# A graph network on one core: rows of y scattered behind later gathers, and the hub's scores turned through two PSUM banks

## The chip, the cores and the metric

The kernel runs on one core of a Trainium2 chip. The time is the device time of one launch in microseconds, from the first to the last instruction with what lies around it. The kernel before has a median of 2826.6 us in three runs (2820.92 to 2831.66). One execution was taken by the hardware profiler; all rows below are from it, in microseconds from the start of its span.

## What is computed

The graph has 8192 nodes with 128 features and a 0/1 adjacency matrix of 8192 x 8192 with ones on its diagonal. Its first nodes have many neighbours and its last ones a few.

```python
def reference(x, adj, W0, b0, a_s, a_r, W1, b1):
    # layer 0: attention over the neighbours
    h = maximum(layernorm(x), 0)
    H = h @ W0.T + b0
    s, r = H @ a_s, H @ a_r
    e = leaky_relu(adj * s + adj * r.T, 0.2)
    x = x + softmax(where(adj > 0, e, -9e15), axis=1) @ H
    # layer 1: sum over the neighbours, then the largest over the neighbours
    h = maximum(layernorm(x), 0) @ W1
    p = maximum(adj @ h + b1, 0)
    return x + max_over_neighbours(p, adj)
```

Below, y is `layernorm(x)` of layer 1 after its maximum, times W1: one row of y per node.

## The kernel before

The 8192 rows are 64 tiles of 128. Tile 0, the hub, is dense and has its own path; the other 63 are sparse. **Layer 0** reads the adjacency matrix tile by tile in the order STREAM, packs each row's bits on TensorE (`pack`), and VectorE takes the numbers of the neighbours out of them (`extract`). Rows are then sorted by their number of neighbours in four groups (`rank_group` on POOL, behind VectorE's ranks), so that tile q of the ranked order needs A_SLOTS[q] gathers: each gather (L589) is one indirect DMA of 128 rows of `h_table` into a slot of the ring of 64 slots.

All engines run the same list of steps, n = 0 to 76, and meet by semaphores. STEP[q] says at which step ranked tile q is scored. In step n ScalarE normalizes the tiles of step n - 2 (`tile_normalize`), copies their transposes (`tile_copies`, L790), writes their rows of y (`tile_rows`, L803), then makes the raw scores of this step's tiles (`raw_scores`, L747). VectorE finishes scores (L1314, which gathers four tiles later wait for), and TensorE sums the slots one step later (`sum_slots`, L976).

POOL's order is written out: for q = 0 to 62 the gathers of tile q, and behind them the scatters (L602) of the tiles m with BEHIND[m] = q. Before the tiles 0, 16, 27 and 47 it ranks a group (L575). A scatter of tile m waits for the row of y of step STEP[m] + 2; a gather of tile q waits for the scores of tile q - 4 and for free slots. POOL works in order, so what stands behind a waiting scatter waits with it.

The hub's scores are made by VectorE in steps 64 to 67 and become exponents on ScalarE. In the steps 68 to 71 they are turned and multiplied in 16 chunks of 4 blocks, four chunks a step. For chunk c TensorE transposes four blocks into PSUM (`dense_transpose`, L1016), ScalarE copies them to SBUF (`dense_keep`, L817) and TensorE multiplies them with 512 rows of `h_table` (`dense_sum`, L1023), which SP loads (L437) into one of two buffers once the sum two chunks before is done. The order on TensorE is transposes of c, then sum of c - 1. Step 72 closes the hub (`dense_close`, L1370 on) and gives its row of y.

**Layer 1** then splits y in three bf16 parts (`split_y`, L1392 on), multiplies the packed words of tiles 1 to 27 and the hub on TensorE (L1093), while POOL gathers y for the rest (L624); at last POOL gathers the results (L661) and VectorE takes the largest (L1330).

Of the kernel before, what the change touches and what calls it, by code (L numbers as in the profile page):

```python
# [7 lines left out]
ALU, ACT, AX = mybir.AluOpType, mybir.ActivationFunctionType, mybir.AxisListType  # L8

P = 128  # L10
# [6 lines left out]
BANK = 512  # L17
VSCALE = 4096.0
BATCH = 4
BATCHES = T // BATCH  # L20
# [69 lines left out]
def gathered_by(slots):  # L90
# [21 lines left out]
STEP = [18, 19, 20, 20, 21, 22, 22, 23, 24, 24, 25, 25, 26, 26, 27, 27, 34, 38, 40, 41, 42, 43, 44, 45, 46, 46,  # L112
    47, 53, 54, 55, 55, 56, 57, 57, 58, 58, 59, 60, 60, 61, 61, 62, 62, 63, 63, 64, 64, 65, 66, 67, 68, 68,
    69, 69, 70, 70, 71, 71, 72, 72, 73, 73, 74]
BEHIND = [5, 6, 8, 8, 9, 11, 11, 12, 14, 14, 16, 16, 17, 17, 17, 17, 20, 21, 23, 24, 25, 26, 27, 27, 30, 30, 31,
    32, 33, 35, 35, 36, 38, 38, 40, 40, 41, 44, 44, 47, 47, 47, 47, 49, 49, 51, 51, 52, 53, 54, 56, 56, 58,
    58, 61, 61, 62, 62, 62, 62, 62, 62, 62]
HUB_SCORES, HUB_SUMS, HUB_NORM = T, T + 4, T + 8
LAST = max(STEP[-1] + 2, HUB_NORM + 1)
AT_STEP = {n: [q for q in range(NR) if STEP[q] == n] for n in range(-3, LAST + 1)}  # L120
SCATTER_BEHIND = {n: [q for q in range(NR) if BEHIND[q] == n] for n in range(NR)}

# [39 lines left out]
def build(nc, x, adj, W0, b0, a_s, a_r, W1, b1, out):  # L162
    ctx = ExitStack()
    with ctx:
        def sb(name, shape, dt=F32):
            return ctx.enter_context(nc.sbuf_tensor(name, shape, dt))

        def ps(name, shape, dt=F32):
            return ctx.enter_context(nc.psum_tensor(name, shape, dt))

        def sem(name):
            return ctx.enter_context(nc.semaphore(name))
# [13 lines left out]
        a_buf = sb("a_buf", [P, 2, N])  # L186
# [47 lines left out]
        ident = sb("ident", [P, P])  # L234
# [31 lines left out]
        hn = [sb(f"hn{i}", [P, BATCH, D]) for i in range(2)]  # L266
        hT = [sb(f"hT{i}", [P, BATCH, P]) for i in range(2)]
# [51 lines left out]
        psV = [ps(f"psV{i}", [P, WORDS]) for i in range(2)]  # L319
        psF = ps("psF", [P, BANK])  # L320
        psW = psF[:].bitcast(BF16)
        psT = ps("psT", [P, BATCH, P])
        psH = [ps(f"psH{i}", [P, BANK]) for i in range(2)]
        psA = [psV[i][:, 0:BANK] for i in range(2)]

        s_xin, s_w, s_b1, s_c0, s_c1, s_c2, s_const, s_waug, s_waug_sb, s_held, s_constants = (
# [29 lines left out]
        s_hin, s_htr, s_hwt, s_hmm, s_hst = (  # L356
            [sem(f"{n}{l}") for l in range(3)] for n in ("s_hin", "s_htr", "s_hwt", "s_hmm", "s_hst"))
# [323 lines left out]
        def _(act):  # L681
# [131 lines left out]
            def dense_keep(l, t, c):  # L813
                act.wait_ge(s_htr[l], t * BATCHES + (c + 1))
                if c >= 2:
                    act.wait_ge(s_hmm[l], t * BATCHES + (c - 1))
                act.activation([hn[1], hT[1]][c % 2][:].rearrange("p u n -> p (u n)"), psF[:], ACT.Copy).then_inc(  # L817
                    s_hwt[l], 1)

            def dense_norm(l, t):  # L820
# [13 lines left out]
            for n in range(LAST + 1):  # L834
# [33 lines left out]
                if HUB_SUMS <= n < HUB_NORM:  # L868
                    for c in range(4 * (n - HUB_SUMS), 4 * (n - HUB_SUMS) + 4):
                        dense_keep(0, 0, c)  # L870
# [23 lines left out]
            with act.If(general(act) > 0):  # L894
                with act.Fori(0, T) as t:
                    dense_exponents(1, t)
                    for c in range(BATCHES):
                        dense_keep(1, t, c)
                    dense_norm(1, t)
                with act.Fori(0, T) as t:  # L900
                    for c in range(BATCHES):
                        dense_keep(2, t, c)

        @block.tensor
        def _(pe):
# [101 lines left out]
            def dense_transpose(l, t, c):  # L1007
                if l == 2:
                    pe.wait_ge(s_hin[2], (t + 1) * 16)
                else:  # L1010
                    pe.wait_ge(s_hexp[l], t * PLANES + (c // 2 + 1))
                if c >= 1:
                    pe.wait_ge(s_hwt[l], t * BATCHES + c)
                for j in range(BATCH):
                    at = (c * BATCH + j) * P
                    last = pe.transpose(psF[:, j * P:(j + 1) * P], a_buf[:, 0, at:at + P], ident[:])  # L1016
                last.then_inc(s_htr[l], 1)

            def dense_sum(l, t, c):
# [15 lines left out]
            for n in range(LAST + 1):  # L1035
# [26 lines left out]
                if HUB_SUMS <= n < HUB_NORM:  # L1062
                    if n == HUB_SUMS:
                        pe.wait_ge(s_wt, DENSE)
                        pe.wait_ge(s_onehot, 4)
                    for c in range(4 * (n - HUB_SUMS), 4 * (n - HUB_SUMS) + 4):
                        dense_transpose(0, 0, c)
                        if c > 0:
                            dense_sum(0, 0, c - 1)
# [13 lines left out]
            for c in range(DENSE_BATCHES):  # L1083
                if c >= 2:
                    pe.wait_ge(s_relu, c - 1)
                for i, b in enumerate(BLOCK_ORDER):
# [3 lines left out]
                    for k in range(PLANES):  # L1090
                        at = (b * PLANES + k) * D
                        for part in range(3):
                            last = pe.matmul(psA[c % 2], y_part[part][:, at:at + D],  # L1093
                                             bit_rows[(c * BLOCKS + i) % 3][:, k, :],
                                             start=(i == 0 and k == 0 and part == 0),
                                             stop=(i == BLOCKS - 1 and k == PLANES - 1 and part == 2))
# [7 lines left out]
            with pe.If(general(pe) > 0):  # L1104
                with pe.Fori(0, T) as t:
                    for c in range(BATCHES):
                        dense_transpose(1, t, c)
                        if c > 0:
                            dense_sum(1, t, c - 1)
                    dense_sum(1, t, BATCHES - 1)  # L1110
                    dense_norm(1, t)
                with pe.Fori(0, T) as t:
                    for c in range(BATCHES):
                        dense_transpose(2, t, c)
                        if c > 0:
                            dense_sum(2, t, c - 1)
                    dense_sum(2, t, BATCHES - 1)
# [497 lines left out]
```

## Time and profile before

| | us |
|---|---|
| median of 3 runs | 2826.6 |
| lowest, highest | 2820.92, 2831.66 |
| the profiled execution | 2835.18 |
| its span | 2826.0 |
| mean granted TensorE clock | 0.669 |

A row of the order of time gives start, duration, engine, line, operation, output and input, the number of instructions merged in it, and in brackets how long the engine stood idle before it and what released it. "issue" means that nothing was waited for that the profile shows; "remote" that the releaser isn't known. The ends of matmuls are modelled.

### The profile page before, as it was taken

How to read it: one execution, taken by the hardware profiler on the slowest of the kernel's cores; microseconds unless marked ns; L12 is line 12 of the kernel's file. 1: busy time of each engine (PE TensorE's matmuls, PEld its weight loads, DVE VectorE, ACT ScalarE, POOL GpSimd, SP SyncE). 2: the span in 40 equal slices, each digit the busy share in tenths (PEclk: the TensorE clock that was granted, in tenths of full speed). 3: DMA queues.
4: the chain of work that ended last, by engine and by line, in shares of the span. 5: the costliest groups of instructions: out<-in, count | busy, mean ns of one | idle time of the engine just before them, and what ended most of it. 6: DMA issues, size and time to landing. Idle time of an engine off the chain costs nothing.

```text
span 2826.0 us, 19035 instructions
## 1 busy us (share of the span) xinstructions
PE 968.4 (34%) x4534; PEld 535.7 (19%) x4534; DVE 1438.5 (51%) x3301; ACT 456.3 (16%) x1519; POOL 1562.0 (55%) x1616
## 2 busy tenths in 40 slices
PE   3664156525245536423539996600000000000000
PEld 1431133213122213323514432300000000000000
DVE  6888677855334525443265543547656345222222
ACT  1631145302123214433410000000000000000000
POOL 0102755444664645576363564677766755677776
PEclk8987577767677768666759997855555555555555
DMA  9999668788567879632441221152232111222121
GB/s 351 410 381 375 189 239 291 283 224 321 194 241 244 297 261 387 212 79 70 120 97 40 75 61 48 51 132 59 67 56 43 52 42 40 48 57 54 49 47 41
DMA packets 155983, 447.42 MB, mean 158 GB/s; under 512 B 34557, under 2 KB 81459, under 8 KB 122970
## 3 DMA queue, kind: packets, MB, share of 16 engines
q1 hardware_dynamic: 80506, 311.94, 29.2%
q0 software_dynamic: 53184, 114.44, 16.9%
q10 hardware_dynamic: 22176, 19.77, 2.3%
q8 instruction: 38, 0.62, 0.1%
q14 instruction: 79, 0.65, 0.1%
HBM read 408.06 MB, written 37.95 MB: 158 GB/s over the span
## 4 chain that ended last, share of the span: by engine, by line
another core or an unknown queue 20%; POOL 18%; PE 16%; issue 15%; DVE 11%; DMA 6%; DVEq 6%; ACT 4%; SPq 2%; ACTq 1%; POOLq 0%
POOL ring L661 16%; PE psV L1093 9%; DMA a_buf<-in_adj 5%; PE psV L920 3%; DVE squares L1330 2%; SPq L390 2%; ACT ring L764 2%; POOL out L667 1%; PE psH L976 1%; DVE a_buf L1495 1%; DVEq L1499 1%; DVE words L1221 1%; DVE words L1212 1%; DVEq L1215 1%
## 5 line engine op out<-in xcount | busy, mean ns | idle before, releaser
L589 POOL DMA_INDIRECT ring<-h_table,srec x518 | 506.5, 978 | 304.0 <-issue 170.3
L661 POOL DMA_INDIRECT ring<-p_table,srec x545 | 529.8, 972 | 200.3 <-issue 166.9
L920 PE MATMUL psV<-a_buf,bit_ident 128*128 128x512 bf16 x1024 | 318.4, 476 | 245.7 <-DMA a_buf<-in_adj 173.8
L1330 DVE TENSOR_REDUCE squares<-ring 128x128 f32<-128x640 f32 (+15 forms) x99 | 178.0, 1798 | 333.4 <-DMA ring<-p_table,srec 301.9
L976 PE MATMUL psH<-ring,ident 128*128 128x128 f32 x1036 | 159.3, 316 | 205.9 <-remote 93.2
L624 POOL DMA_INDIRECT ring<-y_table,srec x198 | 191.8, 969 | 62.4 <-issue 61.8
L1093 PE MATMUL psV<-rec_all,a_buf 128*128 128x512 bf16 x888 | 202.0, 385 | 26.0 <-issue 25.9
L1103 PE MATMUL psH<-ones_row,flag_col 128*1 128x1 f32 x2 | 0.2, 163 | 589.7 <-DVEq L1556 589.7
L920 PEld LDWEIGHTS psV<-a_buf,bit_ident 128*128 128x128 bf16 x1024 | 115.5, 115 | 432.3 <-issue 296.0
L976 PEld LDWEIGHTS psH<-ring,ident 128*128 128x128 f32 x1036 | 149.6, 228 | 220.2 <-issue 205.9
L1314 DVE SCALAR_TENSOR_TENSOR e_sc<-e_sc 128x6 f32<-128x6 f32 (+19 forms) x63 | 10.7, 170 | 259.1 <-ACT e_sc L748 245.0
L764 ACT ACTIVATE ring<-ring,prob 128x128 f32<-128x128 f32 x433 | 131.9, 389 | 5.4 <-issue 3.9
L1458 DVE TENSOR_SCALAR rec_all<-a_buf 128x512 uint16<-128x512 uint16 x296 | 67.6, 301 | 122.7 <-remote 73.9
L1093 PE MATMUL psV<-wbuf,a_buf 128*128 128x512 bf16 x456 | 113.6, 399 | 47.5 <-issue 25.9
L575 POOL DMA_INDIRECT records<-rec_all,rank x63 | 61.4, 974 | 98.6 <-DVEq L1302 80.6
L1212 DVE MAX8 words<-psV 128x8 f32<-128x1024 f32 x63 | 77.7, 1233 | 71.9 <-remote 49.4
L1093 PEld LDWEIGHTS psV<-rec_all,a_buf 128*128 128x128 bf16 x888 | 87.6, 99 | 136.8 <-issue 36.1
L1103 PEld LDWEIGHTS psH<-ones_row,flag_col 128*1 128x1 f32 x2 | 0.1, 80 | 590.0 <-issue 590.0
L661 POOL DMA_INDIRECT ring<-p_table,w_aug x93 | 87.8, 944 | 36.0 <-issue 28.0
L631 POOL DMA_INDIRECT p_table<-rec_all,srec x36 | 35.8, 994 | 123.3 <-DVEq L1447 117.7
L564 POOL DMA_DIRECT2D h_table<-stage x16 | 12.3, 766 | 160.6 <-ACT rs_col L713 160.6
L602 POOL DMA_INDIRECT y_table<-rec_all,srec x36 | 36.0, 1001 | 116.9 <-ACT rec_all L803 110.8
(228 smaller groups left out, 2055.5 us busy)
## 6 DMA issues: line engine op xcount, KB each, us to landing
a_buf<-in_adj SPq DMA_DIRECT2D x256, 1024.0 KB
ring<-p_table,srec POOLq DMA_INDIRECT x545
ring<-h_table,srec POOLq DMA_INDIRECT x518
trec<-records ACTq DMA_DIRECT2D x63, 128.5 KB
packed<-wbuf ACTq DMA_DIRECT2D x28, 256.0 KB
a_buf<-packed SPq DMA_DIRECT2D x7, 1024.0 KB
h_table<-stage POOLq DMA_DIRECT2D x16, 258.0 KB, 7.6
a_buf<-r_row SPq DMA_DIRECT2D x1, 4096.0 KB
```

Of the source, the lines that this page charges most:

```text
L390: sp.dma_start(a_buf[:, n % 2, cols], adj[STREAM[n] * P:(STREAM[n] + 1) * P, cols]).then_inc(s_a[n % 2], 16)
L575: pool.indirect_dma_start(records[g], bass.IndirectOffsetOnAxis(rank[:, g, i:i + 1], 0), rec[g][:, i, :], None).then_inc(s_rec, 16)
L589: pool.indirect_dma_start(ring[:, A_AT[q] + j, :], None, h_table, bass.IndirectOffsetOnAxis(srec_u[g][:, i, LIST + j:LIST + j + 1], 0)).th ...
L624: pool.indirect_dma_start(ring[:, Y_AT[m] + j, 0:D], None, y_table, bass.IndirectOffsetOnAxis(srec_u[g][:, i, LIST + j:LIST + j + 1], 0)). ...
L661: pool.indirect_dma_start(ring[:, C_AT[n] + j, 0:D], None, p_table, bass.IndirectOffsetOnAxis(slot, 0)).then_inc(s_rows[n % BUFS], 16)
L764: act.activation(row, row, ACT.Copy, scale=prob[q % 2][:, j:j + 1])
L920: last = pe.matmul(psV[n % 2][:, h * BANK:(h + 1) * BANK].rearrange("p (g n) -> p g n", n=P), bit_ident[:, k, :], rows[:, :, k, :], start= ...
L976: pe.matmul(psH[q % 2][:, 0:D], ident[:], ring[:, A_AT[q] + j, 0:D], start=(j == 0), stop=False)
L1093: last = pe.matmul(psA[c % 2], y_part[part][:, at:at + D], bit_rows[(c * BLOCKS + i) % 3][:, k, :], start=(i == 0 and k == 0 and part == 0 ...
L1212: dve.max(words[:, 0:8], src)
L1330: dve.tensor_reduce(to, ring[:, at:at + n, 0:D].rearrange("p s d -> p d s"), AX.X, op)
L1458: last = dve.tensor_scalar(bit_rows[n % 3][:, k, :].bitcast(U16).rearrange("p (u n) -> p u n", n=P), words_in[c % 2][:, :, b * P:(b + 1) * ...
```

## The change

The list BEHIND is changed for 18 tiles: the scatters of the tiles 7 to 9, 31 to 38 and 49 to 55 stand behind the gathers of later tiles, by 2 to 49 gathers. Tiles 8 and 9 go past the second ranking to behind tile 16, tiles 37 and 38 past the fourth ranking to behind tile 47.

In the hub's chunks the transposes of even chunks go to the bank psF as before and those of odd chunks to the first bank of psV[1]. The transposes of chunk c wait for the copy of chunk c - 2 instead of that of chunk c - 1.

```diff
-BEHIND = [5, 6, 8, 8, 9, 11, 11, 12, 14, 14, 16, 16, 17, 17, 17, 17, 20, 21, 23, 24, 25, 26, 27, 27, 30, 30, 31,
-    32, 33, 35, 35, 36, 38, 38, 40, 40, 41, 44, 44, 47, 47, 47, 47, 49, 49, 51, 51, 52, 53, 54, 56, 56, 58,
-    58, 61, 61, 62, 62, 62, 62, 62, 62, 62]
+BEHIND = [5, 6, 8, 8, 9, 11, 11, 13, 16, 16, 16, 16, 17, 17, 17, 17, 20, 21, 23, 24, 25, 26, 27, 27, 30, 30, 31,
+    32, 33, 35, 35, 37, 39, 39, 41, 41, 44, 47, 47, 47, 47, 47, 47, 49, 49, 51, 51, 52, 53, 56, 58, 58, 61,
+    61, 62, 62, 62, 62, 62, 62, 62, 62, 62]
...
+        psX = [psF, psV[1]]
...
-                act.activation([hn[1], hT[1]][c % 2][:].rearrange("p u n -> p (u n)"), psF[:], ACT.Copy).then_inc(
+                act.activation([hn[1], hT[1]][c % 2][:].rearrange("p u n -> p (u n)"), psX[c % 2][:, 0:BANK], ACT.Copy).then_inc(
...
-                if c >= 1:
-                    pe.wait_ge(s_hwt[l], t * BATCHES + c)
+                if c >= 2:
+                    pe.wait_ge(s_hwt[l], t * BATCHES + c - 1)
                 for j in range(BATCH):
                     at = (c * BATCH + j) * P
-                    last = pe.transpose(psF[:, j * P:(j + 1) * P], a_buf[:, 0, at:at + P], ident[:])
+                    last = pe.transpose(psX[c % 2][:, j * P:(j + 1) * P], a_buf[:, 0, at:at + P], ident[:])
```

## Rows read from the trace of the kernel before

**Rows 1.** The page: busy time of each engine, and the chain that ended last.
```profile
PE 968.4 (34%) x4534; PEld 535.7 (19%) x4534; DVE 1438.5 (51%) x3301; ACT 456.3 (16%) x1519; POOL 1562.0 (55%) x1616
...
another core or an unknown queue 20%; POOL 18%; PE 16%; issue 15%; DVE 11%; DMA 6%; DVEq 6%; ACT 4%; SPq 2%; ACTq 1%; POOLq 0%
```
**Rows 2.** Table of stretches: us, busy per engine, TensorE clock, DMA share, GB/s.
```profile
1448.00:1855.00 407.00, 313.08 (x1372) 136.59 (x1370) 190.09 (x601) 8.58 (x14) 221.24 (x228) 0.86 0.23 62
1855.00:2826.00 971.00, 0.19 (x2) 0.11 (x2) 407.92 (x508) 0.00 (x0) 676.78 (x695) 0.50 0.23 54
```
**Rows 3.** POOL in order of time, 1317 to 1390 us.
```profile
1317.43 0.94 POOL L589 DMA_INDIRECT ring<-h_table,srec  x1 [0.30 <-issue]
1332.43 0.98 POOL L602 DMA_INDIRECT y_table<-rec_all,srec  x1 [14.06 <-ACT rec_all L803]
...
1342.48 0.94 POOL L589 DMA_INDIRECT ring<-h_table,srec  x1 [0.30 <-issue]
...
1380.89 0.94 POOL L589 DMA_INDIRECT ring<-h_table,srec  x1 [0.30 <-issue]
```
**Rows 4.** ScalarE in order of time, the hub's copies, 1321 to 1384 us.
```profile
1321.34 0.60 ACT L817 ACTIVATE hn<-psF 128x512 f32<-128x512 f32 x1 [12.99 <-remote]
...
1334.99 0.57 ACT L817 ACTIVATE hn<-psF 128x512 f32<-128x512 f32 x1
1336.69 0.60 ACT L817 ACTIVATE hT<-psF 128x512 f32<-128x512 f32 x1 [1.13 <-PE psF L1016]
...
1345.23 0.60 ACT L817 ACTIVATE hT<-psF 128x512 f32<-128x512 f32 x1 [4.40 <-remote]
...
1383.02 0.60 ACT L817 ACTIVATE hT<-psF 128x512 f32<-128x512 f32 x1 [5.76 <-remote]
```
**Rows 5.** Waits of 1302:1430 (us, times, longest); then L790: what ended ScalarE's idleness.
```profile
ACT hT L817 <- remote: 15.3, 3, 5.8
...
  remote: 143.4, 15
```
**Rows 6.** TensorE and SP in order of time, 1307 to 1325 us.
```profile
1307.51 1.91 PE L1023 MATMUL psV<-stage,hn 128*128 128x128 f32 x8
1309.21 1.06 PE L1016 MATMUL psF<-ident,a_buf 128*128 128x128 f32 x4
...
1321.28 0.91 SPq L437 DMA_DIRECT2D stage<-h_table  x2
...
1324.24 2.04 PE L1023 MATMUL psV<-stage,hn 128*128 128x128 f32 x8 [1.07 <-DMA stage<-h_table]
```
**Rows 7.** POOL: two scatters and two rankings in time, then waits of 1110:1192 and 1302:1392.
```profile
480.06 0.98 POOL L602 DMA_INDIRECT y_table<-results,srec  x1 [3.98 <-ACT results L803]
499.25 0.97 POOL L602 DMA_INDIRECT y_table<-results,srec  x1 [6.95 <-ACT results L803]
518.12 0.98 POOL L575 DMA_INDIRECT records<-rec_all,rank  x1 [12.80 <-DVEq L1302]
...
1195.99 0.99 POOL L575 DMA_INDIRECT records<-rec_all,rank  x1 [2.65 <-DVEq L1302]
...
POOL y_table L602 <- ACT rec_all L803: 22.5, 5, 8.8
...
POOL y_table L602 <- ACT rec_all L803: 36.6, 4, 14.1
```
**Rows 8.** ScalarE and VectorE in order of time: scores of later tiles.
```profile
1246.10 0.32 ACT L747 ACTIVATE e_sc<-ring,srec 128x14 f32<-128x14 f32 x1 [14.10 <-DMA ring<-h_table,srec]
...
1264.32 0.17 DVE L1314 SCALAR_TENSOR_TENSOR e_sc<-e_sc 128x9 f32<-128x9 f32 x1 [2.45 <-issue]
...
1333.29 0.17 DVE L1314 SCALAR_TENSOR_TENSOR e_sc<-e_sc 128x6 f32<-128x6 f32 x1 [24.34 <-ACT e_sc L748]
```
**Rows 9.** VectorE and TensorE in order of time, from the hub's close to layer 1.
```profile
1394.54 0.16 DVE L1370 TENSOR_REDUCE hub_inv<-hub_l 128x1 f32<-128x8 f32 x1
...
1447.89 2.72 PE L1093 MATMUL psV<-wbuf,a_buf 128*128 128x512 bf16 x6 [20.97 <-DVE wbuf L1458]
```

## The prediction

> **What bounds the kernel now.** I read the page first, then the table of stretches, then the order of time engine by engine. The page says that no engine is full: POOL is busy for 55% of the span, VectorE for 51%, TensorE for 34% [rows 1]. The chain of the page splits in the same way, with a fifth of it put down to nothing that the profile can name [rows 1]. So the change has to be judged where it works, and the rest of the kernel counts only as something that is shifted. The table of stretches shows this: from 1855 us to the end only POOL and VectorE work, POOL for 677 of 971 us, and TensorE's long stage lies between 1448 and 1855 us [rows 2]. Neither holds an edited instruction. They begin when layer 0 is done, so what the change is worth is what it does to the end of layer 0, the hub's close and the first product of layer 1.
>
> That start is set by the hub. Its close on VectorE begins at 1394.54; behind it come the hub's row of y, the loads of y and twelve splits on VectorE before the first unpacking, and TensorE starts at 1447.89 [rows 9]. Ahead of 1394.54 stand the steps 68 to 71, each with four chunks of the hub's scores. Once in each of them ScalarE's copy waits for something that the profile can't name: 12.99 us in step 68, and 15.3 us in three waits in the steps 69 to 71 [rows 4, 5]. I read these waits beside POOL's order. The last gather of a run ends at 1318.37 (1317.43 + 0.94), 1343.42 and 1381.83 [rows 3], and the copies start at 1321.34, 1345.23 and 1383.02 [rows 4], 2.97, 1.81 and 1.19 us later. Step 70 looks alike. Layer 0 as a whole has 15 more such waits at L790, 143.4 us of ScalarE [rows 5]. TensorE's own records of the work waited for are much earlier: the third group of transposes is drawn at 1309.21 with 1.06 us, the copy that waits for it starts at 1321.34, and SP's loads, of which one waits for the sum drawn at 1307.51, leave at 1321.28 [rows 4, 6]. Two engines agree on the late time, so the late time is the real one. The Trainium skill (Perfetto Trace Analysis, the per-instruction lifecycle of the Tensor Engine) says that the end drawn for TensorE is an estimate; by that reading the trace agrees, the lag here being 11 us.
>
> **The change part by part.**
> *The hub's banks.* No operation is added or removed: 64 transposes and 16 copies stay. Before, a group of transposes waits for the copy of the group ahead, and the copy then waits for the transposes: the copy at 1334.99 takes 0.57, and the next one starts at 1336.69 [rows 4]. With two banks the transposes of an odd chunk are done ahead, and the second copy can follow at once: 1336.69 - 1335.56 = 1.1 us per step at most, for the pair that isn't held. But the sum of a chunk still waits for its rows: the load that leaves at 1321.28 lets the sum start at 1324.24 [rows 6], two chunks behind. And the last copy of steps 68 to 71 is held by the unnamed wait in any case. From below zero I exclude: psV[1] is free from step 64 on, as TensorE waits for the last turned words. Bounds 0 and 4 x 1.1 = 4.4 us of gain; I take 1, because three of four steps end in the unnamed wait, and in step 71 I expect part of it to be free.
>
> *The rows of y.* 18 scatters move behind 2 to 49 later gathers. On POOL that takes away 11 waits: 3.98 and 6.95 us in the first group, five with 22.5 us in the third, four with 36.6 us in the fourth, 70.0 us in all [rows 3, 7]. Each scatter is still 0.98 us and each gather 0.94, with 0.30 between them, near 1.3 and 1.25 us [rows 3], so POOL's work is the same. Where do the 70 us go?
> In the first group the wait is followed by one for VectorE's ranks, 12.80 us before the first record of the second group [rows 7]: the gain ends there, 0. In the third group there is the same wait, 2.65 us [rows 7]; ranks come from step 62, and step 62 isn't reached sooner by gathers that already run two steps ahead of the scores. I take 0 with bounds of -3 and +3, the wait that can be used up.
> Scatters 37 and 38 move past the fourth group's ranks to behind gather 47, where four others stand already. That puts 2 x 1.3 = 2.6 us ahead of gather 48. Rows are waited for here: ScalarE stood 14.10 us before tile 47's, and VectorE 2.45 us before the score of tile 48, with only hub scores behind it [rows 8]. This cost is on the path: +2.6.
> In the fourth group a gather still waits for the score of the tile four before it. So POOL doesn't run away: without the scatter of tile 49 it goes on to gather 55 (4 gathers, 5.0 us) and then stands before gather 56 until the score of tile 52, made at 1333.29, 0.9 us behind the scatter's start at 1332.43 [rows 3, 8]. If TensorE's completion comes only behind the run of gathers, then that run now ends 5.0 us later in step 68: +5.0. In step 69 the run is four gathers, a scatter and four gathers as before (11.3 us) but starts behind the score: with the drain and POOL's own start I take +1.5. In step 70 it is three gathers, two scatters, three gathers, 10.1 instead of 11.35 us, and starts later by the same: +0.3. In step 71 it is five gathers and two scatters, 8.9 instead of 12.6 us: -3.7 + 1.5 = -2.2.
> Sum: 2.6 + 5.0 + 1.5 + 0.3 - 2.2 = +7.2, less 1 for the banks: +6.2 us. The profiled execution has a span of 2826.0 us and took 2835.2 us, 0.3% above the median of 2826.6 us; a shift of 6 us carries over whole, so 2826.6 + 6 = about 2832 us.
>
> A rule speaks against the reading on which this rests. The Trainium skill (SBUF — State Buffer, "Who interferes with whom") says that a DMA written by POOL is held only by VectorE's shared port and that a DMA never contends with another engine. By it TensorE's late completions have nothing to do with the runs, and a longer run costs nothing, which is the second rival. The rows above don't agree with it, as far as a coincidence of three times can tell.
>
> **The rivals.**
> *The waits turn into time.* The 36.6 us that POOL loses in the fourth group are real idle time of the engine that otherwise holds TensorE. If gathers done early leave TensorE alone when the hub's chunks come, each of the four steps loses part of its unnamed wait, 12.99 us and 15.3 us in three [rows 4, 5]. Two thirds of step 68's and half of the others would be 8.7 + 7.6 = 16 us: 2826.6 - 16 = 2811. For it: those waits are large. Against it: the score of the tile four back keeps POOL's work inside the same steps.
> *Nothing is coupled.* The unnamed waits have another origin and stay; POOL's waits were free. Then only the banks act, 3 us of the 4.4, and scatters 37 and 38 hide: 2824. Against it: the runs' ends and the waits' ends lie together too often. For it: nothing that I know of makes TensorE wait for POOL's DMAs.
> *Slower.* The hold isn't given back. Where a run grows, TensorE's sums that begin in it wait for its end: tile 13's gathers (5, 6.25 us) before scatter 7, tile 37's (5, 6.25 us) before scatter 31, tile 55's (5.0 us) before scatter 49, and 2.6 us for scatters 37 and 38: 20 us, 2847. It decides from the point where later runs, though shorter, end no sooner, because their start hangs on the score, which itself comes behind the hold.
> *The change doesn't do what it says.* VectorE and ScalarE keep TensorE from using the second bank and the scatters wait where the gathers did: 2827.
>
> **How the numbers follow.** Coupled, with the hold given back in part (2832): 0.50. Nothing coupled (2824): 0.20. Waits turn into time (2811): 0.14. Slower (2847): 0.12. No effect (2827): 0.04. The median's own spread is 2820.9 to 2831.7. For 8 in 10 the range has to reach over the centre of the fast rival and most of the slow one: 2811 to 2846. About 0.5% (14 us) is what a measurement of this kernel can tell from no change. Faster by more than that: over half of the fast rival, 0.09. Slower: three quarters of the slow one and the tail of the forecast, 0.12. Between them 0.79.
>
> **What would show it.** The run behind gather 54 goes on with gather 55, and the copy of step 68 that stood at 1321.34 comes 5 to 8 us later, again behind the last gather. POOL's waits ahead of L602 in the fourth group shrink below 15 us and stand ahead of L589 instead, with the scores as releaser. VectorE's hub close moves from 1394.54 to about 1401, TensorE's first product from 1447.89 to about 1454. In the first pair of a step's hub copies the second follows the first within 0.1 us, where it took 1.1 us. It would be wrong if those copies come in the middle of a run of gathers, if the third group's ranks move by more than 3 us, or if anything behind 1455 us changes its length.

## The result and the profile after

The changed kernel has a median of 2835.55 us in 20 runs (2820.82 to 2842.82), the kernel before 2827.38 us in 20 runs. The ratio is 1.0023 with a 95% interval of 1.0013 to 1.0033: 6.5 us slower, between 3.7 and 9.3 (the two medians lie 8.2 us apart). The forecast was +6.2 us, about 2832 us. The profiled execution took 2841.26 us, its span is 2833.2 us, against 2835.18 and 2826.0 us before. Line numbers of the changed kernel are higher by 1.

The page of the changed kernel, busy times and the chain that ended last, as [rows 1]:

```profile
PE 973.4 (34%) x4534; PEld 537.1 (19%) x4534; DVE 1438.1 (51%) x3301; ACT 457.0 (16%) x1519; POOL 1566.3 (55%) x1616
...
issue 20%; POOL 19%; PE 17%; another core or an unknown queue 12%; DVE 11%; DMA 6%; DVEq 5%; ACT 5%; SPq 4%; ACTq 1%; POOLq 0%
```

The busy times are within 5 us of those of before, with the same counts of instructions: nothing was added. The unnamed share of the chain fell from 20% to 12%, and that of "issue" rose from 15% to 20%. Then the two last stretches, as [rows 2] (the second is longer by the longer span):

```profile
1448.00:1855.00 407.00, 310.84 (x1372) 136.21 (x1372) 190.55 (x603) 8.67 (x14) 225.25 (x232) 0.86 0.24 62
1855.00:2833.00 978.00, 0.19 (x2) 0.11 (x2) 407.80 (x508) 0.00 (x0) 675.82 (x692) 0.50 0.23 54
```

POOL in order of time where its list was changed most, as [rows 3]:

```profile
1330.19 0.95 POOL L590 DMA_INDIRECT ring<-h_table,srec  x1 [0.30 <-issue]
1344.69 0.95 POOL L590 DMA_INDIRECT ring<-h_table,srec  x1 [13.55 <-DVEq L1318]
...
1348.44 0.95 POOL L590 DMA_INDIRECT ring<-h_table,srec  x1 [0.30 <-issue]
...
1361.73 0.95 POOL L590 DMA_INDIRECT ring<-h_table,srec  x1 [6.02 <-DVEq L1318]
...
1377.35 0.95 POOL L590 DMA_INDIRECT ring<-h_table,srec  x1 [5.80 <-DVEq L1318]
```

The run goes on to gather 55 and ends at 1331.14; then POOL stands before gather 56 until the score of tile 52. The later runs too begin behind a score. Of the 36.6 us that POOL waited ahead of L602 between 1302 and 1392 [rows 7] nothing is left ahead of its scatters there; it waits 31.1 us ahead of gathers instead, each time for a score. ScalarE's copies beside them, as [rows 4] and [rows 5]:

```profile
1313.66 0.58 ACT L818 ACTIVATE hn<-psF 128x512 f32<-128x512 f32 x1
1314.13 0.59 ACT L818 ACTIVATE hT<-psV 128x512 f32<-128x512 f32 x1
1334.70 0.60 ACT L818 ACTIVATE hn<-psF 128x512 f32<-128x512 f32 x1 [19.98 <-remote]
1335.20 0.59 ACT L818 ACTIVATE hT<-psV 128x512 f32<-128x512 f32 x1
...
1345.20 0.58 ACT L818 ACTIVATE hn<-psF 128x512 f32<-128x512 f32 x1
...
1350.35 0.60 ACT L818 ACTIVATE hT<-psV 128x512 f32<-128x512 f32 x1 [2.29 <-remote]
...
1357.70 0.45 ACT L791 ACTIVATE hT<-psT 128x128 f32<-128x128 f32 x2 [3.47 <-remote]
...
1368.84 0.60 ACT L818 ACTIVATE hT<-psV 128x512 f32<-128x512 f32 x1 [4.08 <-remote]
...
1381.64 0.60 ACT L818 ACTIVATE hT<-psV 128x512 f32<-128x512 f32 x1 [1.25 <-PE psV L1017]
```

In step 68 the unnamed wait grew from 12.99 to 19.98 us and again ends behind the run, by 3.56 us. In the steps 69 to 71 the hub's share of it shrank: 15.3 us in three waits became 2.29 + 4.08. Another 3.47 us stand now ahead of the copies for the rows of y (L791), where this stretch had none before; they end 2.0 us behind the run whose last gather ends at 1355.71. So part of the wait only changed its place. The odd copies follow the even ones by 0.5 us, start to start. VectorE's hub close and TensorE's first product, as [rows 9], moved by 0.4 and 0.3 us only, where 6 to 7 us had been forecast for both:

```profile
1394.94 0.16 DVE L1371 TENSOR_REDUCE hub_inv<-hub_l 128x1 f32<-128x8 f32 x1
...
1448.19 6.64 PE L1094 MATMUL psV<-wbuf,a_buf 128*128 128x512 bf16 x24 [21.10 <-DVE wbuf L1459]
```

So in this pair of executions 6.8 of the 7.2 us between the spans lie behind the close: 2826.0 - 1394.54 = 1431.5 us before, 2833.2 - 1394.94 = 1438.3 after. The hub's steps began 7.75 us later (1313.66 against 1305.91) and were 7.35 us shorter together. One execution of each can't say whether that is the change; the runs below say how much this stretch varies.

### The profile page after: what moved, and what is told of

The parts are those of the page before. It is cut to its first block, busy times and chain, and to the rows that moved or that the text cites. A ratio compares the mean times of both kernels' runs of the same rounds, so it can differ in the third digit from the quotient of the medians.

```text
span 2833.2 us, 19034 instructions
## 1 busy us (share of the span) xinstructions
PE 973.4 (34%) x4534; PEld 537.1 (19%) x4534; DVE 1438.1 (51%) x3301; ACT 457.0 (16%) x1519; POOL 1566.3 (55%) x1616
## 4 chain that ended last, share of the span: by engine, by line
issue 20%; POOL 19%; PE 17%; another core or an unknown queue 12%; DVE 11%; DMA 6%; DVEq 5%; ACT 5%; SPq 4%; ACTq 1%; POOLq 0%
POOL ring L662 15%; PE psV L1094 10%; DMA a_buf<-in_adj 4%; PE psV L921 2%; DVE squares L1331 2%; SPq L391 2%; PE psH L977 2%; POOL out L668 1%; ACT ring L765 1%; SPq L404 1%; DVE a_buf L1496 1%; DVEq L1500 1%; DVE a_buf L1486 1%; POOL records L576 1%
## 5 line engine op out<-in xcount | busy, mean ns | idle before, releaser
L921 PE MATMUL psV<-a_buf,bit_ident 128*128 128x512 bf16 x1024 | 326.6, 485 | 236.3 <-DMA a_buf<-in_adj 145.9
L1213 DVE MAX8 words<-psV 128x8 f32<-128x1024 f32 x63 | 77.7, 1233 | 60.0 <-remote 49.3
L668 POOL DMA_INDIRECT out<-results,srec x63 | 64.1, 1018 | 52.1 <-DVEq L1532 33.8
```

The costliest lines, as they stand in the source:

```text
L668: pool.indirect_dma_start(out, bass.IndirectOffsetOnAxis(srec_u[g][:, i, ROW:ROW + 1], 0), results[:, n % RESULTS, :], None).then_inc(s_re ...
L921: last = pe.matmul(psV[n % 2][:, h * BANK:(h + 1) * BANK].rearrange("p (g n) -> p g n", n=P), bit_ident[:, k, :], rows[:, :, k, :], start= ...
L1213: dve.max(words[:, 0:8], src)
```

## The experiments

The experiments were run in four groups on three chips, and these are of two kinds: on two of them the kernel before takes 2485 us, on the third 2853 us; on that of the first pair it took 2827 us. Each ratio is against the kernel before, run on the same chip at the same time. The lists BEHIND are given by the tiles whose scatters are at their new place.

**The banks alone (e1), the list alone (e2), the tiles 7 to 9 alone (e3), 49 to 55 alone (e4).**

```diff
# e1: psX as in the change, BEHIND as before
# e2: BEHIND as in the change, psF alone as before
# e3: only these of BEHIND
-..., 12, 14, 14, ...   (tiles 7, 8, 9)
+..., 13, 16, 16, ...
# e4: only these of BEHIND
-..., 54, 56, 56, 58, 58, 61, 61, ...   (tiles 49 to 55)
+..., 56, 58, 58, 61, 61, 62, 62, ...
```

> The hub's two banks alone, BEHIND as before. The theory on record gives -1 us, with -4.4 as its bound: the median within 0.15% of the kernel before, the second hub copy of a step within 0.1 us behind the first where 1.1 us lay between them, and the last copy of the steps 68 to 70 still 1 to 3 us behind POOL's last gather. If nothing is coupled, -3 us. If the banks matter otherwise (copies or transposes in each other's way) it is slower by more than 2 us.

> The list BEHIND alone, the hub's chunks through one bank. The theory on record gives +7.2 us. If nothing is coupled, 0. If the banks carry the 0.2% of the whole change, this one is at 0 as well; if the scatters carry it, this one stands at +0.2% to +0.3%.

> Only the scatters of the tiles 7, 8 and 9 are moved. The theory on record gives 0: the time won is lost again in the wait for the second group's ranks. The profile of the whole change says otherwise: there the first record of the second group came 3 us later, and the gathers behind it 5 to 6 us later. If that belongs to these three scatters, the ranks come 3 to 6 us later here too, and the time is +0.1% to +0.2%. If it was the scatter of one execution, ranks and time are as before.

> Only the scatters of the tiles 49 to 55 are moved. The theory on record gives +4.6 us (5.0 + 1.5 + 0.3 - 2.2): the copy of step 68 comes 5 us later behind gather 55, and the hub's close 4 to 5 us later. The profile of the whole change says otherwise: there the hub's steps began 7.8 us late and the close came 0.4 us late, so the steps 68 to 71 gave 7 us back. If that belongs to these scatters, close and time here are 4 to 7 us earlier than before (-0.15% to -0.25%); if the banks gave it back, e1 shows it and this one is at +0.15% or at 0.

Before 2484.59 us. e1: 0.9986 (0.9976 to 0.9996). e2: 1.0014 (1.0003 to 1.0024). e3: 1.0002 (0.9991 to 1.0012). e4: 1.0010 (0.9998 to 1.0022). On this chip the banks gain 3.5 us, as the rival "nothing is coupled" had it (3 us). But the list costs as much, where that rival had 0. The moved tiles 7 to 9 cost nothing that can be told from noise, and neither the cost nor the gain that e4's expectation named for the tiles 49 to 55 is clear of it.

**The kernel before again (e5), the whole (e6), the tiles 37 and 38 alone (e7).**

```diff
# e7: only these of BEHIND
-..., 44, 44, ...   (tiles 37, 38)
+..., 47, 47, ...
```

> The kernel before itself, for its trace on the chip of these runs. If TensorE's late completions behind POOL's runs of gathers belong to the kernel, ScalarE's copies in the steps 68 to 71 stand again 0.3 to 3 us behind the last gather of a run, with unnamed waits of 28 us in those steps, and TensorE issues one product per 2.8 us at the beginning of layer 1. If they belong to the chip of the first profile, and this is the chip of e1 to e4 (2485 us), there are no unnamed waits and the products follow each other by 0.2 us.

> The whole change again. On the chip of the first pair (2827 us) it was +0.23%. If the parts of e1 to e4 add up on their chip (banks -0.14%, the list +0.14%), it is at 0 +-0.15% here, with the banks giving back what the list costs. If the parts don't add up, it stands at +0.2% as on the first chip.

> Only the scatters of the tiles 37 and 38 are moved, past the fourth group's ranks to behind gather 47. The theory on record gives +2.6 us (+0.1%): two scatters of 1.3 us more ahead of gather 48, on the path. If the rows of tile 48 aren't waited for, 0; if the ranks come earlier because POOL no longer waits for these rows ahead of them, -2 to -5 us.

Before 2484.50 us; e5 is one run of it, 2484.18 us. e6: 0.9998 (0.9989 to 1.0007): here the whole change is worth nothing, as e1 and e2 add up to. e7: 1.0007 (0.9998 to 1.0017). The trace of e5 is the telling one. ScalarE's hub copies, the same code as [rows 4], and POOL beside them:

```profile
1127.74 0.58 ACT L817 ACTIVATE hn<-psF 128x512 f32<-128x512 f32 x1
1129.59 0.60 ACT L817 ACTIVATE hT<-psF 128x512 f32<-128x512 f32 x1 [1.27 <-PE psF L1016]
1132.15 0.60 ACT L817 ACTIVATE hn<-psF 128x512 f32<-128x512 f32 x1 [1.96 <-PE psF L1016]
1133.56 0.60 ACT L817 ACTIVATE hT<-psF 128x512 f32<-128x512 f32 x1 [0.81 <-PE psF L1016]
```

```profile
1128.77 1.30 POOL L589 DMA_INDIRECT ring<-h_table,srec  x1 [0.30 <-issue]
1130.37 1.04 POOL L589 DMA_INDIRECT ring<-h_table,srec  x1 [0.31 <-issue]
1131.72 0.94 POOL L589 DMA_INDIRECT ring<-h_table,srec  x1 [0.30 <-issue]
1132.97 0.98 POOL L602 DMA_INDIRECT y_table<-rec_all,srec  x1 [0.30 <-issue]
1134.27 0.96 POOL L589 DMA_INDIRECT ring<-h_table,srec  x1 [0.32 <-issue]
```

Four copies in 5.8 us, in the middle of a run of POOL's DMAs of 0.94 to 1.30 us, and the three that waited were released by TensorE by name. In the summary of what ended ScalarE's idleness before a line, first the hub's copies (L817) in the kernel before on the chip of the first pair, then on this one:

```profile
  remote: 28.3, 4
  PE psF L1016: 11.9, 7
```

```profile
  PE psF L1016: 11.3, 12
```

In layer 0 of e5, from 240 us on, no engine has an unnamed wait at all; before had 143.4 us of them at L790 [rows 5]. In layer 1 it is the same. TensorE's products (line L1093) of the kernel before while POOL gathers y, on the first chip and in e5:

```profile
1461.88 0.38 PE L1093 MATMUL psV<-rec_all,a_buf 128*128 128x512 bf16 x1 [1.72 <-issue]
1464.68 0.38 PE L1093 MATMUL psV<-rec_all,a_buf 128*128 128x512 bf16 x1 [2.43 <-issue]
```

```profile
1248.31 10.52 PE L1093 MATMUL psV<-rec_all,a_buf 128*128 128x512 bf16 x47
1258.67 5.34 PE L1093 MATMUL psV<-wbuf,a_buf 128*128 128x512 bf16 x24
```

One product in 2.8 us there, one in 0.22 us here (5.34 / 24). That TensorE is held while POOL works through a run is seen with this kernel on one kind of chip and not on the other, so it isn't a property of the kernel alone. The clock doesn't make the two kinds: TensorE's mean granted clock is 0.669 in the trace of before and 0.689 in e5, but its busy time differs by 51 us only (968.4 and 917.2), of 344 us between the spans.

**The banks and the tiles 31 to 36 (e8); layer 1's gathers later (e9).**

```diff
# e9, against the kernel before
             for m in range(len(Y_SLOTS)):
+                if m == 0:
+                    pool.wait_ge(s_bitsfree, 2)
                 gather_y(m)
```

> Both banks and only the scatters of the tiles 31 to 36 moved: the whole change without the tiles 7 to 9, 37, 38 and 49 to 55. On chips of 2485 us, if the parts measured so far add up (banks -0.14%, tiles 49 to 55 +0.10%, 37 and 38 +0.07%, 7 to 9 +0.02%, the whole -0.02%), the third group is worth -0.07% and this one stands at -0.2%: ahead of both kernels. If the third group is worth nothing, -0.14%. On a chip of 2827 us the theory of held completions gives 0 to -1 us (the record's 0 for the third group and -1 for the banks).

> The kernel before, but POOL's first gather of y in layer 1 waits until TensorE has finished the first two blocks (48 products) of the first tile. Theory of TensorE held by POOL's gathers: on a chip of 2827 us the products 48 and on, which came one per 2.8 us during POOL's run, come at 0.22 us each until POOL starts. On a chip of 2485 us, where the products already follow each other at 0.22 us beside POOL's gathers, nothing changes on TensorE in the first 48 products, and POOL is 20 to 25 us later; of that its wait of 23 us ahead of its first row of p hides nearly all.

Before 2484.93 us. e8: 0.9988 (0.9979 to 0.9997), as the banks alone: the third group is worth nothing here. Against e6 it lacks the tiles 7 to 9, 37 and 38 and 49 to 55, and gains 1.4 us up to step 68 and 3.4 us in the steps 68 to 71 (56.0 against 59.4, in the table below); the times differ by 2.5 us. The traces of e1 to e4 point the same way. With one bank these four steps take 58.1 to 60.4 us with the tiles 49 to 55 at their old place (e3, e5, e7) and 59.6 and 62.2 moved (e2, e4); with two banks 56.0 and 56.5 (e1, e8) against 59.4 (e6). So on this kind of chip, without any hold, the later scatters of the fourth group seem to take back about 3 us of what the banks give; with one bank their cost is lost in the spread. Why they cost anything there is not shown. e9: 2491.51 us in one run. Its POOL starts at 1253.07 instead of 1224.99; TensorE has 24 products in 5.34 us as in e5. But VectorE stood 12.63 us for the rows of y and did its next unpacking late, and TensorE waited 6.20 us for that. The chip was not of the kind on which this run could have shown the hold, so the direct trial of it in layer 1 is still open. And of the 28 us more of POOL's start 6 to 7 came out at the end: the expected cover of 23 us was not all that counted, VectorE's order was the rest.

**The banks and 49 to 55 (e10), the whole without 37 and 38 (e11), the whole without 49 to 55 (e12).**

```diff
# e10: psX, and of BEHIND only the tiles 49 to 55 as in the change
# e11: the change, but with
-..., 47, 47, ...   (tiles 37, 38)
+..., 44, 44, ...
# e12: the change, but with
-..., 56, 58, 58, 61, 61, 62, 62, ...   (tiles 49 to 55)
+..., 54, 56, 56, 58, 58, 61, 61, ...
```

> Both banks and the scatters of the tiles 49 to 55. So far on chips of 2485 us: banks alone -0.14%, banks with the third group -0.12%, the whole -0.02%. If the fourth group takes away what the banks give, as the hub's steps of the whole say (R3 to the close 171.7 us, against 166.8 with the banks and the third group), this one is at 0 to -0.05%, and its time from the fourth ranks to the close is 3 us longer than with the banks alone. If it is the scatters 37 and 38 that take it away, this one is at -0.12%. On a chip of 2827 us the theory of held completions gives here the shorter holds of the steps 69 to 71 of the whole change: 6 to 10 us less from the fourth ranks to the close than before, and -0.2% or more.

> The whole change without the tiles 37 and 38, which stay behind gather 44. Their price by the record is 2.6 us, by the traces on chips of 2485 us 1.4 us from the fourth ranks to step 68 (112.3 against 110.9): the time is 0.06% to 0.1% below that of the whole change, so -0.08% to -0.1% here. If their price is hidden, -0.02% as the whole.

> The whole change without the tiles 49 to 55, which stay where they were. If the fourth group takes away the banks' gain on chips of 2485 us, this one is at -0.1%; the scatters 37 and 38 alone then keep it from -0.15%. If the fourth group costs nothing, -0.02% as the whole. On a chip of 2827 us the holds of the steps 68 to 71 are those of the kernel before (17.3, 10.2, 9.5 and 11.5 us from a step's first hub copy to its last), so nothing is given back and it stands at +0.2% to +0.4%.

These ran on the other kind of chip, before 2852.72 us. e10: 0.9984 (0.9972 to 0.9995). e11: 1.0019 (1.0007 to 1.0030). e12: 1.0008 (0.9997 to 1.0019). e10 was expected at -0.2% or more on a chip with the hold, with 6 to 10 us less from the fourth ranks to the close than before; it came at -0.16%, with 4.6 us less (193.9 against 198.5 in the first pair's trace of before; there is no trace of before on this chip). The expectation of e11 was written for 2485 us, and there is no run of the whole on this chip; e12 was expected at +0.2% to +0.4% and came lower. Between e10 and e11 lie only the tiles 7 to 9 and 31 to 36: 1.0019 - 0.9984 = 0.35%, 10 us, for two groups that the prediction had at 0. Between e12 and e11 the tiles 49 to 55 move and 37 and 38 move back: 1.0019 - 1.0008 = 0.11%, about 3 us slower, on the edge of what these runs can tell.

The tiles 7 to 9 in the traces: ScalarE in order of time around the scatter of tile 7: the kernel before and e10 (scatters 7 to 9 in their old place), then the changed kernel and e12 (moved), each the copy before a row of y (L790, L791):

```profile
477.76 0.28 ACT L790 ACTIVATE hT<-psT 128x128 f32<-128x128 f32 x1 [1.06 <-PE psT L998]
```

```profile
479.84 0.28 ACT L791 ACTIVATE hT<-psT 128x128 f32<-128x128 f32 x1 [1.24 <-PE psT L999]
```

```profile
485.47 0.28 ACT L791 ACTIVATE hT<-psT 128x128 f32<-128x128 f32 x1 [8.05 <-remote]
```

```profile
485.17 0.28 ACT L791 ACTIVATE hT<-psT 128x128 f32<-128x128 f32 x1 [8.30 <-remote]
```

And POOL of the changed kernel: the last gather of the joined run of the tiles 12 and 13, and the scatter of tile 7.

```profile
482.14 1.16 POOL L590 DMA_INDIRECT ring<-h_table,srec  x1 [0.30 <-issue]
487.77 0.99 POOL L603 DMA_INDIRECT y_table<-results,srec  x1 [4.48 <-ACT results L804]
...
521.10 0.98 POOL L576 DMA_INDIRECT records<-rec_all,rank  x1 [22.74 <-DVEq L1303]
```

With scatter 7 between them, POOL pauses behind tile 12 and TensorE's completion comes in the pause, at 477.76. Without it ten gathers follow each other (470.81 to 483.3), and the copy comes 2.2 us behind their end. Of the 6.25 us of tile 13's run 2.5 stay: from scatter 6 to the ranks 49.3 us before and 49.2 in e10, 51.6 after, 51.8 in e11 and e12. On the chips of 2485 us the same distance is 41.9 to 42.6 us with these scatters at their old place (e1, e4, e5, e7, e8) and 41.9, 42.2 and 43.4 moved (e3, e6, e2): no clear cost where there is no hold.

The stretches from the traces of all runs but e9, worked out from starts of records (us; "hold" is the sum over the steps 68 to 71 of the time from the first hub copy of a step to its fourth):

```
                       scatter 6  gather 36  ranks 4     step 68  69    70    71    hold  close
                       to ranks 2 to ranks 4 to step 68                             to end
first pair, 2827 us
 before                49.3       88.1       109.9       29.1     18.7  17.9  23.0  48.5  1419.2
 whole                 51.6       88.2       112.6       31.5     16.7  15.6  17.4  37.7  1426.0
2853 us
 e10 banks, 49-55      49.2       85.4       111.0       32.3     16.8  15.7  18.1  43.3  1434.4
 e11 no 37, 38         51.8       89.8       110.9       33.1     17.4  16.4  20.0  44.0  1435.1
 e12 no 49-55          51.8       89.7       112.5       29.0     15.4  18.7  21.7  43.4  1426.3
2485 us
 e5 before             42.4       69.6       110.9       15.2     13.3  13.2  18.6  18.4  1289.2
 e1 banks              42.3       70.4       110.9       14.6     12.9  13.1  16.0  16.9  1291.2
 e2 list               43.4       69.8       112.3       15.0     13.7  13.6  17.3  22.7  1289.1
 e3 7-9                41.9       68.1       111.0       15.4     13.8  13.9  17.2  22.4  1291.7
 e4 49-55              42.6       69.8       110.8       15.3     14.7  13.3  19.0  20.6  1290.0
 e7 37, 38             41.9       69.0       112.3       14.9     13.3  13.2  16.7  18.2  1289.7
 e8 banks, 31-36       42.2       68.8       110.8       14.2     13.2  12.7  15.9  18.2  1290.6
 e6 whole              42.2       67.8       112.2       14.3     13.1  13.1  18.8  18.6  1289.8
```

The last column is the time from the close to the last scatter of the output. e10, e11 and e12 have the same code there and differ by 8.8 us. So the 6.8 us by which the first pair differs in it are no more than one execution differs from another, and no cause of them is claimed.

## Why the prediction was right, and where it was not

The time was right, but much of that was luck. The hold on which the prediction rested is seen: on one kind of chip TensorE's completions come behind POOL's runs, and a longer run in step 68 holds them longer (19.98, 20.40 and 20.37 us of unnamed wait with the tiles 49 to 55 moved, in the whole, e10 and e11; 12.99 and 14.65 without, before and in e12). That this hold is what the change costs is not shown. On the chips of 2485 us, where there is no hold, the list alone costs 3.5 us all the same. The list alone was never run on a chip with the hold. The sum of 7.2 - 1 agrees with the time partly by errors that cancel.

Several of the prediction's own signs came out against it in the profiled pair. The close was to move to about 1401 and came at 1394.94, and the first product was to come at about 1454 and came at 1448.19. Of the three signs of being wrong all came: hub copies stand in the middle of POOL's work, the third ranking's first record moved by 5.8 us (921.94 to 927.76) and the fourth's by 5.1 (1195.99 to 1201.11), and the stretch behind the close grew by 6.8 us. The last two may be the difference of two executions, as the table shows for such stretches; then this pair of traces neither bears out the sum nor refutes it.

*Scatters 37 and 38, +2.6.* Gather 48 starts 54.3 us behind the fourth ranks, 51.6 before: +2.7, as costed. At step 68 +1.4 on 2485 us (112.2 and 112.3 in e2, e6 and e7 against 110.8 to 111.0 in the other five) and 1.5 to 2.7 on the others (112.5 and 112.6 against 109.9 to 111.0) are left. Right, a little too large. In the time e7 has +0.07% (-0.02% to +0.17%), which can't be told from 0.

*The fourth group, +4.6 in four steps.* Against e12, which has the banks and the old places, e10 and e11 and the whole give for the steps 68 to 71 on average +3.3, +1.6, -2.8 and -3.2, together -1.1 (single traces, between -3.6 and +2.1). The forecast was +5.0, +1.5, +0.3 and -2.2. Step 68 has the right sign and is too large by 1.7 us: the copy at 1321.34 came at 1334.70, 13.4 us later, of which 7.8 are the later start of the step and 5.6 go with the longer run. Step 69 is right and step 71 a little off. Step 70 failed, by 3.1 us. The failing step is "starts later by the same": the run does start later, behind the score, but the hub's chunks of that step don't start later by as much. Before, the run of step 69 began 2.56 us ahead of the step's first hub copy (1332.43, 1334.99); changed, 0.51 us (1344.69, 1345.20), and in the steps 70 and 71 0.2 us where it was 2.0. So the first three chunks pass, and only the last meets the run. I had counted the late start as a cost alone; it takes the run off the hub's way. That is the part of the first rival (waits turn into time) that is true. The copies at 1350.35, 1368.84 and 1381.64 come in the middle of POOL's work, 1350.35 while a scatter runs, 1368.84 and 1381.64 while a gather runs, the sign that I had named against my reading. That the hold lasts to the end of a run is true for the copy of step 68 and for the rows' copies at 1357.70, and not for these three. What ends it, no run here shows. Whether the group as a whole costs less than the +4.6 of the forecast stays open. The traces say -1.1 for these four steps, but the times say more: e11 over e12 is +3 us on one chip, to which the 1.5 to 2.7 us of the tiles 37 and 38 are to be added, so 4.5 to 5.7 us, uncertain by 3 us and more, and on 2485 us e4 has +0.10% (-0.02% to +0.22%), 2.5 us.

*The banks, -1.* Mis-sized. e1 is -3.5 us (-6.0 to -1.0); on 2853 us the steps 68 to 71 of e12 take 84.9 us together, those of before (another chip, 2827 us) 88.6. Both lie within the bound of 4.4 us, but the argument that the unnamed wait takes most of it doesn't hold: from the start of a step's first copy to that of its second it takes 0.5 us where it took 1.4 to 1.8, in every step, in the pair that isn't held. The banks alone were not run on a chip with the hold, and the times don't settle them: if the fourth group costs 4.5 us or more, the -4.6 us of e10 leave -9 us for the banks, more than any trace shows. The named sign, the second copy at once behind the first, holds: 1313.66 + 0.58 and 1314.13 overlap.

*The first group, 0.* Wrong on the chips with the hold, +2.5 us: "the gain ends there" took the wait of 12.80 us for ranks as cover for later work of POOL. But the ranks themselves were made late, in the three traces with these scatters moved and in neither of the two without; that this comes through the row that VectorE's order waits for is my reading of them. The wait grew to 22.74 us and ended later all the same. The prediction had that mechanism only in the slower rival, at 6.25 us.

*The third group, 0 with bounds of 3.* From gather 36 to the fourth ranks 88.1 and 88.2 us in the first pair, but 85.4 in e10 against 89.8 and 89.7 in e11 and e12: 0 to +4.4 us. The upper value lies beyond the bound, and e11 over e10 in time (10 us, of which 2.5 are the first group) speaks for it. The three traces of 2853 us show where, not why; an experiment with the third group alone on such a chip was not made.

*The sum.* 2.5 + (0 to 4.4) + 2 - 1.1 - 3.7 = -0.3 to +4.1 us from the traces, against 6.5 (3.7 to 9.3) measured for the pair. They meet at the ends only, and 2 to 7 us are not accounted for. The stretch from the second to the third ranks (403.8 and 406.7 us in the first pair, 412.0, 413.6 and 407.2 on 2853 us) and that behind the close vary more than this from execution to execution.

*The rest.* "Nothing behind 1455 changes" can't be judged by the single pair, as said. "Nothing is coupled" (2824 us) doesn't fit the chips with the hold, where the copy of step 68 moved with the end of the run. On those of 2485 us it is right about the banks (-3.5 instead of -3) and wrong about the list (+3.5 instead of 0). The rule of the Trainium skill (SBUF — State Buffer, "Who interferes with whom") that a DMA contends with no engine agrees with e5, where copies follow each other by 1.4 to 2.6 us amid gathers, and not with the late completions of the other kind; but whether these come from contention at all, no run here shows.

No version beats the kernel before by much. The best are the banks alone on 2485 us (0.9986) and the banks with the tiles 49 to 55 on 2853 us (0.9984); neither was measured on the other kind.

## What to carry to other kernels

A scatter that waits in the middle of a run of gathers can be a pause in which other engines' work gets through; taking the wait away joins the runs, so look at what was released in the pause before you count the wait as a gain. When work is moved later, ask what of its neighbours is done by then: a run that starts late may collide with less. And a small sum should be checked term by term on its own kernels, since 0.2% came out right here with one of its five terms (the tiles 37 and 38) close to what the runs showed.

## What the runs showed that I had not expected

The same kernel takes 2484.5 to 2484.9 us on two chips, 2853 us on a third, and took 2827 us in the first pair (its chip isn't known to me), with gathers of the same 0.94 us and 0.30 us between them. In the 240 to 1430 us of the slower trace stand unnamed waits of 143.4, 93.2 and 49.4 us for lines of ScalarE, TensorE and VectorE, in the faster none. A cost of one kind (scatters 7 to 9: 2.5 us) is absent on the other, and the whole change is +0.23% on one and -0.02% on the other. What makes a chip be of one kind or the other, nothing here shows; nor does it show that it is the chip and not its condition at the time, since each slower chip was used once.
